# Six down products of a feed-forward layer computed as seven block products each

## The reference, cut to what matters

```python
xn = layernorm(x)
x  = x + attention(xn) + ffn(xn)          # x: 2048 tokens x 512, one causal head of 512

def ffn(x):                               # w_gate, w_up: 512 x 2048, w_down: 2048 x 512
    h = silu(x @ w_gate) * (x @ w_up)     # 2048 tokens x 2048 hidden channels
    g = h.reshape(..., 512, 4)
    h = g * (the two largest of abs(g) in each four)
    return h @ w_down
```

## Time and profile before

| | |
|---|---|
| median of 3 runs | 789.2 us (789.05 to 789.55) |
| the profiled execution | 788.73 us |
| its span | 786.9 us |
| TensorE busy | 783.3 us, 3518 matmuls |
| VectorE busy | 610.2 us |
| ScalarE busy | 319.0 us |
| GpSimd busy | 16.7 us |

### The profile page before, as it was taken

How to read it: one execution, slowest core, us unless ns; L and a number is a source line. 1 busy time by engine, 2 the same in 40 slices (tenths; PEclk the granted TensorE clock), 3 DMA queues, 4 the chain that set the end, 5 groups by cost and what they waited for, 6 DMA issues and landing times.

```text
span 786.9 us, 9292 instructions
## 1 busy us (share of the span) xinstructions
PE 783.3 (100%) x3518; PEld 648.6 (82%) x3518; DVE 610.2 (78%) x964; ACT 319.0 (41%) x514; POOL 16.7 (2%) x26
## 2 busy tenths in 40 slices
PE   9999999999999999999999999999999999999998
PEld 6888888888888888888888888888888888888887
DVE  6988789678635797689989789898657658659786
ACT  5432250234123473464643634463423424335431
POOL 2011110010000000000000000000000000000000
PEclk9999999999999999999999999999999999999999
DMA  9441704500131543684464352797276163161002
GB/s 325 183 162 55 242 0 184 189 2 1 54 101 35 213 184 111 205 340 176 189 210 181 142 202 93 282 338 291 78 284 260 44 241 136 51 241 55 0 1 107
DMA packets 31611, 121.74 MB, mean 155 GB/s; under 512 B 3088, under 2 KB 3664, under 8 KB 29136
## 3 DMA queue, kind: packets, MB, share of 16 engines
q1 hardware_dynamic: 30272, 119.00, 40.9%
q10 hardware_dynamic: 1296, 2.16, 0.8%
HBM read 77.07 MB, written 44.07 MB: 154 GB/s over the span
## 4 chain that ended last, share of the span: by engine, by line
PE 100%; DVE 0%; issue 0%
PE bank L962 13%; PE bank L963 13%; PE bank L961 13%; PE bank L701 10%; PE bank L699 10%; PE bank L700 10%; PE bank L838 8%; PE bank L1041 7%; PE bank L1042 7%; PE bank L1043 7%; PE bank L903 0%; PE bank L709 0%; PE bank L804 0%; PE bank L771 0%; PE bank L1054 0%; PE bank L1053 0%
## 5 line engine op out<-in xcount | busy, mean ns | idle before, releaser
L961 PE MATMUL bank<-X_hi,wset 128*128 128x512 f32 x448 | 174.4, 389 | 0.0
L963 PE MATMUL bank<-X_hi,wset 128*128 128x512 f32 x448 | 174.3, 389 | 0.0
L962 PE MATMUL bank<-X_lo,wset 128*128 128x512 f32 x448 | 174.3, 389 | 0.0
L961 PEld LDWEIGHTS bank<-X_hi,wset 128*128 128x128 f32 x448 | 84.1, 188 | 17.7 <-issue 0.2
L962 PEld LDWEIGHTS bank<-X_lo,wset 128*128 128x128 f32 x448 | 84.1, 188 | 17.5
L963 PEld LDWEIGHTS bank<-X_hi,wset 128*128 128x128 f32 x448 | 84.1, 188 | 17.3
L1041 PE MATMUL bank<-dw,hs_hi 128*128 128x512 f32 x224 | 87.2, 389 | 0.0
L1042 PE MATMUL bank<-dw,hs_hi 128*128 128x512 f32 x224 | 87.1, 389 | 0.0
L1043 PE MATMUL bank<-dw,hs_lo 128*128 128x512 f32 x224 | 87.1, 389 | 0.0
L1675 DVE TENSOR_TENSOR acc<-bank,acc 128x512 f32<-128x512 f32 x59 | 40.1, 687 | 40.0 <-PE bank L1043 39.6
L699 PE MATMUL bank<-zg,xT 128*128 128x512 f32 (+2 forms) x132 | 49.8, 377 | 0.0
(11 more groups left out here) (259 smaller groups left out, 1444.3 us busy)
## 6 DMA issues: line engine op xcount, KB each, us to landing
w_operands<-wset SPq DMA_DIRECT2D x8, 3584.0 KB, 13.4
wset<-w_operands SPq DMA_DIRECT2D x8, 3584.0 KB, 12.1
wsum<-w_units SPq DMA_DIRECT2D x28, 256.0 KB, 3.8
dw_raw<-L_ffn_w_down SPq DMA_DIRECT2D x14, 512.0 KB, 5.0
xw<-L_attn_x SPq DMA_DIRECT2D x4, 1024.0 KB, 9.6
xt_raw<-x_t SPq DMA_DIRECT2D x8, 512.0 KB, 8.9
xn_t<-xt_raw SPq DMA_DIRECT2D x8, 512.0 KB, 2.8
acc<-resid SPq DMA_DIRECT2D x2, 2048.0 KB, 9.6
```

The costliest lines, as they stand in the source:

```text
L961: pe.matmul(dst[:], u[:, 0, :], x_hi, start=(first and kt == 0), stop=False, skip_group_check=True)
L962: pe.matmul(dst[:], u[:, 0, :], x_lo, start=False, stop=False, skip_group_check=True)
L963: last = pe.matmul(dst[:], u[:, 1, :], x_hi, start=False, stop=(kt == 1), skip_group_check=True)
```

## The change

The products 6 to 11 (`BLOCKED`), done in the units 8 to 13, become `down_blocked(i)`: tokens, hidden channels and outputs are each halved, and seven products of 256x256 by 256x256 blocks take the place of eight. Each is 2x2x3 = 12 matmuls of 256 columns.

- The chosen values' seven operands are made in the unit itself: VectorE does four sums (`operand_sums`) and seven `operand_lo`, ScalarE seven `operand_hi`, each of 128x512 elements. `kept_hi` and `kept_lo` are gone there.
- The weights' seven operands are made ahead, in six pieces `p` of 128x(7x256), each by four sums of 128x256 (`prep_sums`, VectorE), two casts of 128x768 and 128x1024 (`prep_operands_hi`, ScalarE) and two differences of these sizes (`prep_operands_lo`, VectorE). GpSimd's queue loads a piece's weights (0.5 MB) and stores its operands (1.8 MB), one piece after the other. Pieces 0 to 3 lie in the attention. Piece 4 (`PREP_FIRST`) lies in unit 0, piece 5 (`PREP_LATE`) in unit 3. `down_hi`, `down_lo` and their 1 MB loads are gone for the products 6 to 11. `load_blocked` loads 3.5 MB of operands for two products.
- `acc` and the loads and stores of its halves go, apart from those of the last two products. Each product's four tiles are copied from the banks to `staged`, and two DMAs with `accum_op=ADD` on GpSimd's queue add them in the output in HBM, 0.5 MB each. The attention writes its result there and not to `resid_dram`. The copies are VectorE's in the products 0 to 5 (`take_down`), where `add_down` was, and ScalarE's in 6 to 12 (`keep_part`, `keep_down`). `keep_part` makes seven copies for each product. VectorE adds two of its tiles (`sum_staged`).

```diff
@@ block products on TensorE @@
+            def blocked_part(i, k, op, first):
+                dst = down_bank_blocked(k)            # P7, P4: bank 2; P2: bank 7; others: bank 6
+                pe.wait_ge(op_ready, NOP * block_no(i) + op + 1)
+                if i % 2 == 0:
+                    pe.wait_ge(dwop_loaded[0 if op < FIRST_OPS else 1], 16 * (block_no(i) // 2 + 1))
+                for t in range(2):
+                    for r in range(2):
+                        pe.matmul(out_half, s_hi, d_h, ...)
+                        pe.matmul(out_half, s_hi, d_l, ...)
+                        last = pe.matmul(out_half, s_lo, d_h, ...)
+                last.then_inc(part_full, 1)
+            def down_blocked(i):
...
+                blocked_part(i, D_P1, D_A11, True)
...
+                blocked_part(i, D_P7, D_S3, True)
+                pe.wait_ge(part_kept, kept_before + 1)
+                blocked_part(i, D_P6, D_S2, False)
+                blocked_part(i, D_P2, D_A12, False)
+                pe.wait_ge(part_kept, kept_before + 3)
+                blocked_part(i, D_P5, D_S1, False)
+                pe.wait_ge(part_kept, kept_before + 2)
+                blocked_part(i, D_P4, D_A22, False)
+                pe.wait_ge(part_kept, kept_before + 5)
+                blocked_part(i, D_P3, D_S4, False)
@@ ScalarE, unit n @@
                 nc.scalar.activation(g_sum[3][:], bank[0][:], ACT.Silu).then_inc(silu_ready, 1)
+                if n == 0:
+                    prep_operands_hi(PREP_FIRST, 0)   # waits for the piece's four sums
+                    prep_operands_hi(PREP_FIRST, 1)
...
+                if i in BLOCKED:
+                    operand_hi(i, D_S1)
+                    keep_part(i, D_P1)
+                    operand_hi(i, D_A22)
                 last_silu(n)
-                if n == 2:
+                if i in BLOCKED:
+                    keep_part(i, D_P7)
+                    keep_part(i, D_P6)                # waits for pair_added[1] of product i-1
+                    operand_hi(i, D_S4)
+                    keep_part(i, D_P2)
+                    keep_part(i, D_P5)
+                    keep_part(i, D_P4)
+                    magnitudes(i + 1, (0, 1))
+                    keep_part(i, D_P3)
@@ VectorE, unit n @@
                 add_sum(0, n, bank[4], F_P7, g_sum[2], 3)
+                if i in BLOCKED:
+                    operand_lo(i, D_A11)
                 add_sum(1, n, bank[5], F_P7, b_tile(n, 1), 3)
+                if i in BLOCKED:
+                    operand_sums(i)
...
                 nc.vector.tensor_tensor(b_tile(n, 0)[:], g_sum[3][:], bank[1][:], ALU.mult).then_inc(hid_ready, 1)
+                if n == 0:
+                    prep_sums(PREP_FIRST, 0)
+                    prep_sums(PREP_FIRST, 1)
+                if i in BLOCKED:
+                    operand_lo(i, D_A12)
                 if n < N_Q - 1:
                     last_block(n)
+                if n == 0:
+                    prep_operands_lo(PREP_FIRST, 0)
+                    prep_operands_lo(PREP_FIRST, 1)
+                elif n == 3:
+                    prep_sums(PREP_LATE, 0)
+                    prep_sums(PREP_LATE, 1)
+                if i in BLOCKED:
+                    operand_lo(i, D_S1)
+                    operand_lo(i, D_A22)
+                    operand_lo(i, D_S4)
+                    sum_staged(i)
@@ the sums over i @@
+            def take_down(i, t):
+                if t % 2 == 0 and i:
+                    dve.wait_ge(pair_added[t // 2], 16 * i)
...
+                nc.vector.tensor_copy(staged[t // 2][:, t % 2, :], down_bank(i, t)[:]).then_inc(down_taken, 1)
+                    nc.gpsimd.dma_start(out_tiles[tile:tile + 2].rearrange("t p d -> p t d"), staged[b][:], accum_op=ALU.add
+                                        ).then_inc(pair_added[b], 16)
@@ the hand-written list: the pieces 2 and 3 beside the wide attention of the last chunk @@
+    steps += [*u[0:2], *prep_sum[2], u[2], *prep_hi_steps[2], u[3], *rows_of[2][2], ("rows_load", OLD + 8, 0), *rows_of[2][3], ("rows_load", OLD + 9, 0),
+              *prep_lo[2], prep_store[2], prep_load[3], ...
+                     {2: prep_sum[3], 3: [("w_sum", 0, 1), *prep_hi_steps[3]], 4: [*w_hi_steps[2:4], w_lo_steps[2], v_keep[1], *prep_lo[3]],
+                      5: [prep_store[3], prep_load[4], w_lo_steps[3], ("w_store", 0, 0), v_keep[2], X_hi_steps[0]],
```

More of the change, by code:

```diff
@@ L120, in softmax @@
         return order
+    prep_load, prep_store = ([(kind, p, 0) for p in range(2 * N_PREP)] for kind in ("prep_load", "prep_store"))
+    prep_sum, prep_hi_steps, prep_lo = ([[(kind, p, k) for k in range(2)] for p in range(2 * N_PREP)] for kind in ("prep_sum", "prep_hi", "prep_lo"))
     rows_of = {c: [[("rows", n, 0), ("rows_store", n, 0)] for n in range(TC * c, TC * (c + 1))] for c in WIDE}
@@ L352, in attention_ffn @@
         pick_step, picked, hs_hi_ready, hs_ready = sem("pick_step"), sem("picked"), sem("hs_hi_ready"), sem("hs_ready")
-        down_full, added = sem("down_full"), sem("added")
+        down_full, down_kept, down_taken, added = sem("down_full"), sem("down_kept"), sem("down_taken"), sem("added")
+        pair_added = [sem(f"pair_added{b}") for b in range(2)]
         PICK = 11
@@ L1261, in _ @@
                     picks = i >= 0 and n < N_Q - 1
-                    if picks:
+                    if picks and i - 1 not in BLOCKED:
                         magnitudes(i, (0, 1))
@@ L1287, in _ @@
                     operands_hi(n + 1, 1)
-                if n >= 4 and n % 2 == 0:
+                if n >= 4 and n % 2 == 0 and i not in BLOCKED:
                     down_hi(n // 2 - 1)
@@ L1331, in _ @@
                         magnitude(ND - 3, r)
+                    for t in range(TC):
+                        keep_down(i, t)
+                elif 2 < n < N_Q - 1:
+                    if n == 3:
+                        prep_operands_hi(PREP_LATE, 0)
+                        prep_operands_hi(PREP_LATE, 1)
             act.wait_ge(full[1], FILLS * N_Q)
@@ L1646, in _ @@
                     X_lo_half(0, n)
+                elif kind == "prep_sum":
+                    prep_sums(n, k)
+                elif kind == "prep_lo":
+                    prep_operands_lo(n, k)
                 elif kind == "rows" and n < NT - 2:
@@ L1759, in _ @@
                     operands_lo(n + 1, 3)
-                if picks:
+                if picks and i not in BLOCKED:
                     keep(i, 2)
@@ L1764, in _ @@
                     kept_lo(i, 1)
-                if n == NQ:
-                    down_lo(n // 2 - 1, (1,))
-                    kept_lo(i, 2)
-                    kept_lo(i, 3)
                 hidden(n, 2, 1, g_sum[2], b_tile(n, 1))
-                if picks and n != NQ:
+                if i in BLOCKED:
+                    operand_lo(i, D_S3)
+                    operand_lo(i, D_S2)
+                elif picks:
                     kept_lo(i, 2)
@@ L1786, in _ @@
                 if n == NQ - 1:
-                    add_down(i, 0)
+                    take_down(i, 0)
                     second_T4()
                     X_lo_half(1, 0)
-                    add_down(i, 1)
+                    take_down(i, 1)
                     X_lo_half(1, 1)
                     X_lo_half(1, 2)
-                    add_down(i, 2)
-                    for o in range(3, NOP - 1):
+                    take_down(i, 2)
+                    X_lo_half(1, 3)
+                    take_down(i, 3)
@@ L1795, in _ @@
+                    for o in range(4, NOP):
                         X_lo_half(1, o)
-                    add_down(i, 3)
-                    X_lo_half(1, NOP - 1)
                 elif n == 2:
-                    add_down(i, 0)
+                    take_down(i, 0)
                     sums(n + 1)
-                    add_down(i, 1)
+                    take_down(i, 1)
                     for m in range(4):
                         operands_lo(n + 1, m)
-                    add_down(i, 2)
+                    take_down(i, 2)
@@ L1826, in _ @@
                     keep(i + 1, 0)
                     keep(i + 1, 1)
-                    add_down(i, 3)
                     keep(i + 1, 2)
                     keep(i + 1, 3)
-                elif picks:
-                    for t in range(TC):
-                        add_down(i, t)
             def keep_all(i):
```

338 lines of the change are left out of this document (273 added, 65 removed).

## The result

The changed kernel takes 800.86 us (median of 4 runs, 799.14 to 801.51), the kernel before, on the same chip, 789.36 us (789.05 to 789.55). The ratio is 1.0143, with a 95% interval from 1.0125 to 1.016. It is **slower by 1.4%**, where 0.3% faster was forecast. The time lies outside the range of the prediction.

What follows compares the result with a forecast made beforehand. TensorE was taken as the bound, busy 783.3 of 786.9 us. Terms: -4.8 (saving) + 2.1 (unit 0) + 0.1 + 0.1 = -2.5, so 789.2 becomes 786.7 us; range from 0.3 below 784.6 to 789.6.

Steps and rivals of the forecast that it cites:

- The saving: Six blocked down products: 84 matmuls at 120 ns, 10.08 us instead of 10.88 each, 4.8 us saved in all.
- rival 2: New matmuls step at half of 226.7 ns, saving 8.2 us: 783.3 us, chance 0.03.
- Unit 0: Piece 4's sums and casts delay a bank copy, so TensorE waits 2.1 us at unit 1's fill.
- Units 8 to 13: ScalarE's copies keep 0.6 us of cover; 0.1 us lost in unit 8, none in the others.
- Rivals 3 and 4: Adding DMAs late, 791.5 us, chance 0.09; ScalarE's bank copies short of cover by 0.3 us per product, 788.5 us, chance 0.16.
- The pieces in the attention: Pieces 0 to 3 fit into pauses and covers there: no time lost, with 1.1 us left.
- The block T4: Its load runs behind piece 3's store, piece 4's load and unit 0's operand store; 2 us left, 0 lost.
- Unit 3: Piece 5's sums and differences on VectorE delay unit 4's fill by 0 to 0.3 us; 0.1 taken.
- Rival 5: TensorE's clock falls to 1.2 GHz at unit 0's wait, costing 1.5 us more: 788.2 us, chance 0.06.

Runs made afterwards that it cites:

- The kernel before with one line changed: The kernel before, with the rows x + attention stored into the result instead of a tensor of their own: 789.21 us, ratio 1.0002.
- without the pieces: The changed kernel without making the six pieces, its blocked products multiplying stored gate and up operands instead: 786.09 us, ratio 0.996.
- the best version: The changed kernel with all places found repaired, piece 5's sums ending unit 3, its casts and differences ending unit 4: 785.17 us, ratio 0.995.

## Why the prediction was wrong

**The saving: right.** 120.0 ns for each matmul of 256 columns, 10.08 us for each of the products in the units 9 to 13. The first product, in unit 8, takes 10.31 (I had 0.1 us of wait there, measured 0.2). The fills of the units behind take 0.03 us longer each. Measured 4.6, forecast 4.8 - 0.1. The steps of 120.0 and 226.7 ns stood as in the kernel before, so rival 2 is out. By an estimate from the figures that the Trainium skill gives (TensorE: Matmul & The Clock Gate, Back-to-back issue gap) it would have been 7.1. Against the weight loads I had cited one sentence of the Trainium skill (TensorE: Matmul & The Clock Gate, The mechanism). The same section also lets a load run ahead when it goes to a background weight buffer, so it does not speak against this change, and the loads did run beside the matmuls: the busy times of the two are 658 and 785 us of a span of 799.

```profile
587.97 0.28 PE L1210 MATMUL bank<-dwop,op_hi 128*128 128x256 f32 x1
...
597.93 0.28 PE L1212 MATMUL bank<-dwop,op_lo 128*128 128x256 f32 x1
```

**Unit 0: right.** 1.8 us of wait and 2.1 us lost, forecast 2.1, released by ScalarE's copy, with the two casts before it:

```profile
338.01 1.78 ACT L1312 CAST prep<-prep_raw 128x768 fp32r<-128x768 f32 x2 [3.81 <-DVE prep_raw L1665]
339.69 0.62 ACT L1424 ACTIVATE g_sum<-g_sum 128x512 f32<-128x512 f32 x1
340.22 1.06 ACT L1409 COPY bank<-bank 128x512 f32<-128x512 f32 x2
```

**Units 8 to 13: right.** ScalarE's copies of the parts are ended by TensorE, none by a DMA. A copy from a bank by VectorE takes 0.68 us, and the units 2 and 4 to 6 are not longer for it. Rivals 3 and 4 are out: the adding DMAs land after 6.0 us (median, 5.2 to 20.0).

**The pieces in the attention: this step failed.** "Nothing, with 1.1 us left" measured 10.8 us: 3.4 for piece 0 and 7.4 for piece 2. I had traced VectorE's and ScalarE's own pauses, as they stood in the kernel before. I had then written that each microsecond would be TensorE's if the cover were gone, and had not priced that. Three things were missing.
- A pause was taken for cover although its start isn't fixed. Piece 0's pause begins with the landing of row tiles. Counted from `sum_turn` 1, VectorE's row step came 2.2 us later than in the first profile of the kernel before: the row store took 1.7 us longer to complete, and with the piece's load beside it 0.4 us more passed from the row load to the step. The kernel before with one line changed had the first of these too, and lost nothing by it, because the pause was still empty. I had read one profile.
- The row steps behind piece 2's sums feed SyncE's queue. I had counted what the sums delay on VectorE (a maximum, which has time) and not that the next load in SyncE's order, a quarter of unit 0's weights, waits for a row store, and that for VectorE. That load's sums had 0.9 us until TensorE would wait, and came 5.3 us late: 2.8 by the issue, and 2.5 because the load ran beside piece 2's store.
- I had taken the load of each piece for ready when its sums are due. GpSimd's queue holds the load of piece 2 behind the landing of piece 1's store, and the sums waited 6.77 us for it. They began 10.9 us behind `sum_turn` 2, and in the kernel before VectorE's pause ended at 12.2.

**The block T4: wrong by 1 us.** "Two microseconds are left there; I take 0": its load took 6.4 us from issue to cast, and 3.3 before. Piece 4's load, issued at 304.54 behind piece 3's store, and a later store of unit 0's operands (299.56) ran beside it. TensorE waited 0.84 us. **Unit 3: mis-sized.** 0.1 us forecast, 0.9 measured. I had followed piece 5's sums to the pause behind them, and not to the first `take_down`, which stands 1.5 us later in VectorE's order and frees a bank that TensorE wants. **Unit 7: not seen**, 1.7 us, of which 1.0 is there without the pieces too: the adding DMA of product 4 competes with the loads of the second half's blocks (`b_apart` lands 5.7 us after its issue, 4.3 before).

**Rival 5 was real, in another place.** The clock fell behind the waits of 1.67 and 4.40 us. That made 1.7 and 2.8 of the 12.5 us. Behind the wait in unit 0, for which I had priced it at 1.5, it stayed at 1.00 in the changed kernel, and fell in three of the five experiments with the same wait, where it cost 1.7 us.

What stays open: why the stores around 130 to 140 us complete up to 2 us later in some profiles than in others, and 0.7 us between the first two `sum_turn` steps that the best version still loses, 0.3 of them at 175 us, where piece 0's casts delay a cast of `zg`. The start to `sum_turn` 1 is no effect of the change: it is 133.98, 134.24 and 134.61 us in the three profiles of the old order.

## What to carry to other kernels

A pause of an engine is cover only as long as what ends it stays where it is: ask first whether the change moves the transfer or the copy that ends the pause, and whether a second profile has it in the same place. Follow each inserted step past its own engine, to every queue that waits for what stands behind it. Where the order is written out by hand, a DMA queue that serves loads for two purposes in turn is the link through which 1.5 us of sums become 7 us of TensorE's.

## What the runs showed of the hardware

- **Short waits can halve TensorE's clock.** Over all profiles: behind 22 waits of 0.5 to 1.4 us in the stretches where it otherwise works without a pause it never did. Behind waits of 1.8 us it did in three cases of six, and in all cases behind 1.67 and from 2.0 us up (2.04, 2.42, five of 4.1 to 4.4, and 6.81). Each time it cost 1.5 to 3.1 us more, half of the time at the lower level behind the wait. In these kernels a wait of TensorE of 1.7 us cost up to twice its length.
- **A DMA that adds.** GpSimd is busy for 1.21 us with each issue, and 0.5 MB lands 6.0 us after it (median of 26, 5.2 to 20.0).
- **GpSimd's reduction beside VectorE.** In the best version `PARTITION_ALL_REDUCE` began at 169.21 us. The first of a piece's four sums and differences of 128x256 on VectorE, begun 0.47 us behind it, took 1.26 us, and the three behind that 0.41 to 0.43. Two other profiles with this order show the same 1.26. The Trainium skill (SBUF — State Buffer, Who interferes with whom) says that an operation with two inputs in SBUF contends with GpSimd's reads. The trace agrees for the first of the four. The second began and ended at its usual speed inside the reduction's 2.19 us, and the third began there.

```profile
169.68 1.26 DVE L1665 TENSOR_TENSOR prep_raw<-prep_raw 128x256 f32<-128x256 f32 x1
170.86 0.41 DVE L1666 TENSOR_TENSOR prep_raw<-prep_raw 128x256 f32<-128x256 f32 x1
...
169.21 2.19 POOL L808 PARTITION_ALL_REDUCE max_all<-max_one  x1 [19.89 <-DVE max_one L1915]
```
